# State-space stage of a decoder layer: convolution taps read from PSUM, four banks for the input projection, one pass for all step sizes, and a new order of the two halves

## The reference, cut to what matters

```python
h  = x + mamba2(rmsnorm(x))                       # the state-space stage: this case
h2 = h + silu(n @ gate.T) * (n @ up.T) @ down.T   # n = rmsnorm(h), 1792 inner columns; then x is added
# ... layer norm, cross attention with 8 groups, layer norm, low-rank experts, layer norm

def mamba2(x):
    z, xBC, dt = split(x @ w_in.T, [512, 768, 4])
    xBC = silu(depthwise causal conv over 4 tokens of xBC)       # 6 pieces of 128 channels
    xs, Bs, Cs = split(xBC, [128, 128, 512])
    dt = softplus(dt + dt_bias)                                  # a step size per token and head
    cs = cumsum(dt * A); Ldec = tril(exp(cs_i - cs_j))
    Y = ((Cs @ Bs.T) * Ldec) @ (xs * dt) + D * xs                # per batch and head, 128 tokens
    return (Y * silu(z)) @ w_out.T
```

## Time and profile before

| | us |
|---|---|
| median of 3 runs | 1048.18 |
| the runs | 1047.97 to 1050.05 |
| span of the profiled execution, first to last instruction | 1047.3 |
| PE busy in it | 1001.8 (96%) |
| DVE, ACT, POOL busy | 525.8, 513.7, 434.8 |

### The profile page before, as it was taken

How to read it: one execution, slowest core, us unless ns; L and a number is a source line. 1 busy time by engine, 2 the same in 40 slices (tenths; PEclk the granted TensorE clock), 3 DMA queues, 4 the chain that set the end, 5 groups by cost and what they waited for, 6 DMA issues and landing times.

```text
span 1047.3 us, 16399 instructions
## 1 busy us (share of the span) xinstructions
PE 1001.8 (96%) x5232; PEld 831.5 (79%) x5232; DVE 525.8 (50%) x1229; ACT 513.7 (49%) x1809; POOL 434.8 (42%) x386
## 2 busy tenths in 40 slices
PE   5897998999999998999999999999999999999995
PEld 3664686888888887888888888888888888888772
DVE  4879555122221274445454554545454545545676
ACT  4644443222231347655656555655656556555533
POOL 4435737343443454432623534433433434334311
PEclk9999999999999999999999999999999999999996
DMA  6110114110111112000100110110110110100002
GB/s 209 41 41 0 41 56 146 61 48 12 60 60 60 61 41 74 16 30 38 60 28 12 60 40 0 60 40 0 60 40 20 40 40 20 40 0 1 1 1 81
DMA packets 12832, 45.53 MB, mean 43 GB/s; under 512 B 1600, under 2 KB 2112, under 8 KB 9728
## 3 DMA queue, kind: packets, MB, share of 16 engines
q1 hardware_dynamic: 12800, 45.13, 12.3%
HBM read 43.03 MB, written 2.10 MB: 43 GB/s over the span
## 4 chain that ended last, share of the span: by engine, by line
PE 57%; DVE 2%; POOL 1%; ACT 1%; issue 0%; ACTq 0%
PE bank L349 15%; PE bank L351 15%; PE bank L350 15%; PE bank L621 5%; PE bank L631 3%; PE bank L601 3%; PE bank L708 1%; PE bank L608 1%; POOL w_lo L1264 0%; PE bank L717 0%; DVE bst L1728 0%; PE bank L737 0%; DVE res L1948 0%; POOL pb L1433 0%; PE bank L725 0%
## 5 line engine op out<-in xcount | busy, mean ns | idle before, releaser
L349 PE MATMUL bank<-act_hi,w_hi 128*128 128x512 f32 x560 | 225.8, 403 | 3.9 <-ACT cbuf L838 2.3
L351 PE MATMUL bank<-act_hi,w_lo 128*128 128x512 f32 x560 | 220.9, 395 | 0.0
L350 PE MATMUL bank<-act_lo,w_hi 128*128 128x512 f32 x560 | 220.5, 394 | 0.0
L1422 POOL TENSOR_TENSOR qr<-qv,pow_m 128x4 f32<-128x4 f32 x64 | 64.4, 1007 | 172.3 <-DVE qv L1818 171.0
L349 PEld LDWEIGHTS bank<-act_hi,w_hi 128*128 128x128 f32 x560 | 106.5, 190 | 29.3 <-issue 7.3
L350 PEld LDWEIGHTS bank<-act_lo,w_hi 128*128 128x128 f32 x560 | 106.4, 190 | 24.0 <-issue 2.2
L351 PEld LDWEIGHTS bank<-act_hi,w_lo 128*128 128x128 f32 x560 | 106.4, 190 | 23.4
L1433 POOL TENSOR_TENSOR pb<-pb,prec 128x512 f32<-128x512 f32 x64 | 73.4, 1147 | 109.4 <-DVE prec L1838 109.4
L1829 DVE SCALAR_TENSOR_TENSOR pb<-bank,qr,mask_sb 128x128 f32<-128x128 f32 x256 | 71.9, 343 | 74.2 <-PE bank L621 72.9
L349 PE MATMUL bank<-w_hi,ot_hi 128*128 128x512 f32 x256 | 106.5, 416 | 0.7 <-DVE ot_lo L1498 0.7
L1133 ACT ACTIVATE pb<-pb,nmax 128x128 f32<-128x128 f32 x256 | 100.0, 409 | 9.2 <-DVE nmax L1833 9.2
(11 more groups left out here) (178 smaller groups left out, 2129.4 us busy)
## 6 DMA issues: line engine op xcount, KB each, us to landing
raw_a<-in_w_q SPq DMA_DIRECT2D x8, 1024.0 KB, 4.8
raw_b<-in_w_o SPq DMA_DIRECT2D x8, 1024.0 KB, 4.8
raw_a<-in_w_gu SPq DMA_DIRECT2D x7, 1024.0 KB, 5.2
raw_b<-in_w_kv SPq DMA_DIRECT2D x8, 512.0 KB, 3.3
raw_b<-in_w_dn SPq DMA_DIRECT2D x7, 512.0 KB, 3.4
res<-in_x SPq DMA_DIRECT2D x8, 256.0 KB, 6.2
raw_b<-in_ctx_t SPq DMA_DIRECT2D x8, 256.0 KB, 3.9
xre<-in_x SPq DMA_DIRECT2D x2, 1024.0 KB, 6.8
```

The lines of the kernel that those rows point to most:

```text
L349: mm(o, l_hi, r_hi, start=first, stop=False)
L350: mm(o, l_hi, r_lo, start=False, stop=False)
L351: return mm(o, l_lo, r_hi, start=False, stop=last)
L1422: TT(qr[:, 4 * n + h, :], qv[:, 4 * n + h, :], pow_m[:, 0:HALF], ALU.pow).then_inc(qr_done, 1)
```

## The change: what it does

- DVE's three taps read the projection in its PSUM bank, shifted by 1, 2 and 3 tokens, instead of the padded tile; tile `pre`, its memset and ACT's copy into it (L834) are gone. The bank is free only when the taps are done (conv_c), no longer when ACT has read it (conv_ev).
- The projection goes through banks 4, 5, 0, 1 in turn for f = 0 to 11, then 6, 0, 1, 6, 0, 1, 0, 1.
- All step sizes are worked out in one pass on 32 columns, after the second half's dt_step, in bank 7.
- y_out(0) and y_out(3) no longer stand between the taps of a convolution.
- norm_t 4 to 7 move up, in front of in_step 1 to 4; ssm1(0) comes before in_step(10), the others follow one step earlier; out_step(0) and (1) move between the last in_steps, and norm_t 8 to 12 are spread among the out_steps. ACT, POOL and DVE are reordered to go with it.

```diff
+IN_BANK = [4, 5, 0, 1, 4, 5, 0, 1, 4, 5, 0, 1, 6, 0, 1, 6, 0, 1, 0, 1]
...
     def in_step(f):
-        if f >= 2:
-            pn, pp = order[f - 2]
+        if f == 12:
+            pe.wait_ge(dt_ev, 2)
+        elif f >= 4:
+            before = max(e for e in range(f) if IN_BANK[e] == IN_BANK[f])
+            pn, pp = order[before]
             if pp < NCONV:
-                pe.wait_ge(conv_ev, NCONV * pn + pp + 1)
+                pe.wait_ge(conv_c, NCONV * pn + pp + 1)
             else:
...
     def ssm1(b):
         if b:
             pe.wait_ge(xt_ev, b)
+        else:
+            pe.wait_ge(dt_a, 1)
...
             pe.wait_ge(att_done, b - 1)
+        elif b:
+            pe.wait_ge(z_out, 3)
...
     def in_evac(f):
-            if q >= 2:
-                act.wait_ge(conv_c, q - 1)
-            A(pre[:, q % 2, :, DCONV - 1:], bank[f % 2][:, :].rearrange("p (s n) -> p s n", s=HALF),
-              ACT.Copy)
             if q >= 3:
                 act.wait_ge(conv_out, q - 2)
-            A(cbuf[:, q % 3, :], bank[f % 2][:, :], ACT.Identity,
+            A(cbuf[:, q % 3, :], bank[IN_BANK[f]][:, :], ACT.Identity,
...
-    V.memset(pre[:, :, :, :], 0.0).then_inc(setup_v, 1)
...
-    def conv(q, beside=None):
+    def conv(q):
+        raw = bank[IN_BANK[NPIECE * n + p]][:, :].rearrange("p (s n) -> p s n", s=HALF)
         for k in (2, 1, 0):
-            t = STT(c, pre[:, q % 2, :, k:k + L], cw[:, p * DCONV + k:p * DCONV + k + 1], c,
-                    ALU.mult, ALU.add)
+            late = DCONV - 1 - k
+            t = STT(c[:, :, late:], raw[:, :, 0:L - late], cw[:, p * DCONV + k:p * DCONV + k + 1],
+                    c[:, :, late:], ALU.mult, ALU.add)
...
-    def dt_in(n):
-        bias = sp[:, 6, 0:NH].unsqueeze(1).to_broadcast([P, HALF, NH])
+    def dt_in():
+        bias = sp[:, 6, 0:NH].unsqueeze(1).to_broadcast([P, B, NH])
```

More of the change, by code:

```diff
@@ L444, in _ @@
             dt_step(0)
[L445 to L451, removed]
-            dt_step(1)
+            for i in range(4):
+                norm_t(4 + i, (bank[2], bank[3]))
+                in_step(1 + i)
+            in_step(5)
+            dt_step(1)
+            in_step(6)
+            dt_turn()
+            in_step(7)
+            in_step(8)
+            in_step(9)
+            ssm1(0)
             in_step(10)
-            dt_turn(1)
-            ssm1(0)
+            ssm1(1)
             in_step(11)
-            ssm1(1)
-            in_step(12)
             ssm2(0)
             ssm1(2)
-            in_step(13)
+            in_step(12)
             ssm2(1)
             ssm1(3)
+            in_step(13)
+            ssm2(2)
             in_step(14)
-            ssm2(2)
+            ssm2(3)
             in_step(15)
-            ssm2(3)
             in_step(16)
             in_step(17)
+            out_step(0)
             ssm1(4)
             in_step(18)
+            out_step(1)
             ssm1(5)
@@ L474, in _ @@
             ssm2(4)
-            pe.wait_ge(dt_a, 2)
-            out_step(0)
+            out_step(2)
             ssm1(6)
             ssm2(5)
-            out_step(1)
+            pe.wait_ge(z_out, 8)
+            norm_t(8, tb)
+            out_step(3)
             ssm1(7)
+            norm_t(9, tb)
             ssm2(6)
-            out_step(2)
+            out_step(4)
             ssm2(7)
[L484 to L488, removed]
+            norm_t(10, tb)
+            out_step(5)
+            norm_t(11, tb)
+            out_step(6)
+            out_step(7)
             norm_t(12, tb)
@@ L1287, in _ @@
             TT(qk_w[:, :], chan_sb[:, nq:nq + 1], chan_sb[:, nq + 1:nq + 2], ALU.mult).then_inc(setup_p, 1)
-            for p in range(2, 6):
+            rsqrt(4)
+            win_rest(2)
+            rsqrt(5)
+            win_rest(3)
+            win_rest(4)
+            rsqrt(6)
+            win_rest(5)
+            rsqrt(7)
+            for p in range(6, 10):
                 win_rest(p)
             def decay_in(b):
-                pool.wait_ge(dt_done, b // HALF + 1)
+                pool.wait_ge(dt_done, 1)
                 if b == 0:
@@ L1308, in y_rest @@
                 lo(y_lo[:, b % 4, :, :], yb[:, b % 2, :, :], y_hi[:, b % 4, :, :], ylo_done)
-            for i in range(4, 8):
-                rsqrt(i)
-                win_rest(i + 2)
             decay_in(0)
@@ L1349, in _ @@
             decay_in(6)
+            rsqrt(8)
             decay_out(5)
             decay_in(7)
+            rsqrt(9)
+            y_rest(4)
             gu_rest(0, 0)
-            y_rest(4)
             decay_out(6)
-            rsqrt(8)
+            rsqrt(10)
             y_rest(5)
+            gu_rest(0, 1)
             decay_out(7)
-            gu_rest(0, 1)
-            rsqrt(9)
+            rsqrt(11)
+            y_rest(6)
             gu_rest(0, 2)
-            y_rest(6)
-            rsqrt(10)
             y_rest(7)
+            rsqrt(12)
             gu_rest(0, 3)
-            for i in range(11, 16):
+            for i in range(13, 16):
                 rsqrt(i)
@@ L1700, in _ @@
             rms_var(10)
-            y_out(7)
+            att_mul(6)
+            y_out(5)
+            norm_lo(8, tb)
             add_res(3, 3, OUT_BANK[3])
```

199 lines of the change are left out of this document (97 added, 102 removed).

## The result

| | before | after |
|---|---|---|
| median of 10 runs, us | 1048.99 | 1051.79 |
| the runs | 1047.44 to 1050.05 | 1050.27 to 1053.02 |
| ratio after / before, 95% interval | | 1.0022 [1.0014, 1.003] |
| span of the profiled execution | 1047.3 | 1049.8 |
| its stretches, from dt_step(0) on | 38.22, 38.82, 46.77, 901.33 | 39.55, 38.67, 48.63, 901.30 |

The kernel became slower by 0.2%, 2.8 us. The forecast was 1046.0 us, faster than before, in a range from 1042.0 to 1050.8. The first part of the page and the busy time by stretch answer to the earlier trace rows; the cuts are at the same steps (21.65 behind the first in_step, 61.20 behind in_step(9), 99.87 behind in_step(17), 148.50 the first matmul of the MLP).

What follows compares the result with a forecast made beforehand. PE bounds the kernel, paced by DVE in the first 99 us. Stretch terms +0.8, -4.1 and +1.2 gave -2.1 us: span 1045.2, plus 0.9 to the median, stated as 1046.0 us, range 1042.0 to 1050.8.

Steps and rivals of the forecast that it cites:

- 22.0 + 7.3 + 3.4 + 1.9 = 34.7 ... 4.1 less than before: Second stretch: PE's in_steps, ssm1 and ssm2 steps plus 1.9 us lost at ssm2(3), 4.1 us less than before.
- takes 1.4 (0.1 more for POOL's y_rest(1)): Second stretch, DVE's att(3) ahead of conv(9): 1.4 us, with 0.1 more for POOL's subtraction beside it.
- 40.2 + 3.15 + 1.8 + 1.95 = 47.1: Third stretch: PE's work, pause before out_step(0), its clock, wait at ssm2(7); 0.3 us more than before, 2.1 with the clock.
- the first estimate of what is "lost": First three stretches: time beyond PE's own work, 6.0, 5.7 and 6.6 us, 18.3 us that could be won.
- 1.8 us for each pause from 2 us on: PE after a long pause: matmuls at 1.2 GHz for some nine matmuls, counted as 1.8 us more.
- given back: Rival: the second stretch's gain is given back in full by the pauses, each 0.5 us worse; 1048 us, chance 0.12.
- with 0.9 between span and median: Last term of the sum: 0.9 us added to the span of 1045.2 us to get the median, 1046.1 us.
- The first stretch, +0.8: In_steps 0 to 9: 39.0 us, 0.8 more than before, with PE pausing 4.0 us for xn at norm_t(6).
- The taps: DVE's 36 convolution taps read from PSUM: 0.75 us each instead of 1.055, 11 us less DVE work.
- taps unchanged: Rival: the taps cost in PSUM what they cost now; +5 us, 1051.0 us, chance 0.10.
- the late low parts of w_out: Rival: POOL's low parts come later, holding everything from ssm1(4) on; 1050.7 us, chance 0.16.
- fall DVE's way: Rival: DVE wins the port at rms_x(6) and (7), or w_out is split sooner; 1042.5 us, chance 0.22.

Runs made afterwards that it cites:

- din_late: Changed kernel with POOL's decay_in(4) and decay_in(5) moved behind y_rest(2); 1049.53 us, ratio 1.0007.
- three_edits: Changed kernel with xn of batches 6 and 7 made early, y_out(0) to (2) ahead of conv(7) to (9), out_step(0), (1) behind ssm1(4), (5); 1039.14 us.
- out_late: Changed kernel with PE doing ssm1(4) and in_step(18) ahead of out_step(0), and ssm1(5) ahead of out_step(1); 1046.29 us, ratio 0.9976.
- y_first: Changed kernel with y_out(0), (1), (2) on DVE ahead of conv(7), (8), (9) instead of behind them; 1050.37 us, ratio 1.0012.
- xn_early: Changed kernel with the squares, rms_var, rsqrt and rms_x of batches 6 and 7 moved earlier on ACT, DVE and POOL; 1043.81 us, ratio 0.9954.
- taps_alone: Kernel before with the taps from PSUM and the new banks, old order and two step-size passes kept; 1040.59 us, ratio 0.992.
- pool_port: Changed kernel with POOL doing win_rest(5) ahead of rsqrt(6) and win_rest(6) ahead of rsqrt(7); 1051.31 us, ratio 1.003.
- four_edits: Changed kernel with xn early, y_out ahead of conv, out_step(0), (1) behind ssm1, and decay_in(4), (5) behind y_rest(2); 1040.15 us, ratio 0.9904.

## Why the prediction was wrong

**What failed first: the second stretch, "22.0 + 7.3 + 3.4 + 1.9 = 34.7 ... 4.1 less than before".** Measured, 38.67. The step of it was "takes 1.4 (0.1 more for POOL's y_rest(1))". DVE's timeline over two batches:

```profile
77.56 0.69 DVE L1627 TENSOR_TENSOR att<-em,bank 128x512 f32<-128x512 f32 x1 [0.58 <-PE bank L433]
78.29 1.46 DVE L1629 TENSOR_TENSOR att<-att,diag_d 128x512 f32<-128x512 f32 x1
79.67 2.29 DVE L1574 SCALAR_TENSOR_TENSOR cbuf<-bank,cw,cbuf 128x508 f32<-128x508 f32 x3
81.87 0.68 DVE L1637 TENSOR_TENSOR yb<-zt,bank 128x512 f32<-128x512 f32 x1
84.66 1.48 DVE L1629 TENSOR_TENSOR att<-att,diag_d 128x512 f32<-128x512 f32 x1
86.05 2.28 DVE L1574 SCALAR_TENSOR_TENSOR cbuf<-bank,cw,cbuf 128x508 f32<-128x508 f32 x3
88.26 0.68 DVE L1637 TENSOR_TENSOR yb<-zt,bank 128x512 f32<-128x512 f32 x1
```

and POOL's beside it:

```profile
83.29 1.29 POOL L1278 TENSOR_TENSOR y_lo<-yb,y_hi 128x512 fp32r<-128x512 f32 x1 [2.34 <-ACT y_hi L895]
84.55 1.03 POOL L1321 TENSOR_TENSOR md<-dt_sb,cst 128x512 f32<-128x512 f32 x1
```

The walk saw y_rest (until 84.6) and let att's second product go on behind it. But decay_in(5) follows at once, and the product that began at 84.66 took 1.48 us, until 0.56 after decay_in's end. That is 0.75 where 0.1 was counted, and it lies in a loop: y_out, ssm2, att, convolution, y_out. The forecast has 5.5 us for a turn of it; measured, two turns (76.33 to 82.70 and on to 89.08) took 6.4 each. PE has 5.5 us of work in the first of them and only 3.6 in the second, where no ssm1 stands: hence the pauses of 0.70 and 2.53. Behind the second the clock fell, which cost 1.6 more. In din_late, with decay_in elsewhere, the product takes 0.69, a turn 5.6 (75.54, 81.13, 86.73), and the stretch 35.42. Of the 4.0 us that the stretch is too long, then, 0.7 are the first pause, 0.6 the longer second one, 1.6 the clock, and 0.5 PE's own work, which is 33.2 at full clock (three_edits) and not 32.7; the rest is spread.

**What failed with it: the third stretch, "40.2 + 3.15 + 1.8 + 1.95 = 47.1".** It was walked on from in_step(17) ending at 95.85, so din_late, where that nearly came true, is its test: 50.27 us, 3.5 more than before, against +0.3 to +2.1. PE's own work is some 41.5 us and not 40.2 (41.64 busy in three_edits, 41.32 in out_late, both at full clock); the pause before out_step(0) was 3.53 (3.15), its clock 2.5 (1.8), ssm2(7) 1.55 (1.95), and out_step(4) waited 1.23 for add_res, which the walk didn't have. So with the second stretch as forecast the kernel would still not have been faster than before: din_late is at 1049.53, ratio 1.0007 [0.9997, 1.0016]. In the changed kernel the third stretch measured +1.86, inside its range, and that is luck: PE came late, so the pause was only 2.75 with 1.6 of clock, which made up in part for add_res and for PE's work. The low count of PE's work is in the first estimate of what is "lost" as well: of the 6.6 us only some 5.3 were to be had (46.77 less 41.5). The price of a fall of the clock, "1.8 us for each pause from 2 us on", came out at 1.5, 1.6 and 1.6 in the changed kernel, but other runs have pauses over 2 us without a fall (last section).

The rival "given back" had the direction of this, and put it at 1048; in the changed kernel there was no gain in the second stretch to give back. The edits show how far it goes: y_first wins 4.8 and gives 4.4 back, din_late 1.6 of 3.25, xn_early nothing of 6.8.

**The last term, "with 0.9 between span and median".** Every run on record lies 1.8 us above its own span, the changed kernel's median 2.0 above the span of its profile. The 0.9 came from a median of three runs, 1048.18; ten runs give 1048.99. That is 1.1 of the 5.8 us between 1046.0 and 1051.79. The other 4.6 lie in the span: 4.0 in the second stretch, 0.5 in the first, 0.7 in the third, less 0.5 by the earlier start.

**The first stretch, +0.8: measured +1.33, mechanism right.** Xn of batch 6 began at 32.85 (33.35 forecast), took 1.74 with win_rest(5) in its way, PE paused 3.68 (4.0) with the clock low behind it, norm_t(7) 1.12 (1.15), in_step(9) ended at 61.20 (61.1). The stretch is 0.5 longer than forecast because it began 0.5 earlier and still ended where the walk has it. Up to norm_t(7) the distances are the walk's (19.06 us, 18.99 forecast); the 0.5 are lost behind it, where eight transposes took 0.68 (0.35 forecast for the turn) and an in_step 2.77 instead of 2.75. What the walk didn't say is that all this was the price of an order: xn_early takes 6.8 us out of it by moves on three engines.

**The taps: right, and misjudged in their place.** 0.74 us each whatever POOL does, 11.3 us less DVE work as forecast (11). A part of it went to products that POOL now blocks: up to 149 us the 14 xn take 14.7 us (15 took 12.6 before), att's second products 7.6 (6.6). In the old order the taps shorten the first two stretches by 9.3 us (taps_alone). The forecast priced no version without the new order. Measured side by side, the new order with its one pass for the step sizes costs 10.7 us (1051.75 against 1041.05).

**Of the rivals** "taps unchanged" came nearest in time (1051.0), and is out, with taps of 0.74. Next came the late low parts of w_out (1050.7): they did end late, at 102.73 instead of 99.0, but PE was late too, so the pause at out_step(0) was 2.75, not longer than the 3.15. The port did not fall DVE's way (xn took 1.74 and 1.76); pool_port gets a short xn by another order, with the block on conv_silu(1) instead, so what that rival is worth stays unmeasured. None of the three signs that were to show the prediction wrong came (taps of 1.05, no wait at norm_t(6), none at out_step(0)): they watched single mechanisms, and the sum failed.

**Open.** By the ratios against the changed kernel, with some 2 us of doubt on each, xn's place bears 7 us, out_step(0)'s 5 and y_out's 1; together they measured 12. How this compares move by move with the old order was not tried. One pass for all step sizes was not tried alone in the old order, nor the padded tile in the new one. Ssm1(4)'s 2.6 us for conv_silu(11) are still there in the fastest version.

## What to carry to other kernels

Where engines hand a tile round in a loop, add up one turn of the loop, with what the neighbouring engine does next and not only now, and compare it with the bound engine's work in that same turn: 0.75 us of a blocked product decided 3 us here. A gain ahead of a wait is lost at that wait unless what releases it gets earlier too (y_first kept 0.4 of 4.8 us, xn_early all of 6.8), so look for the next releaser and ask where it stands. And price a change that has a cheap part and a reordering separately; here the part alone was worth 0.8%, and the whole cost 0.2%.

## What the runs showed of the hardware

- A DVE operation with two inputs in SBUF that begins while one on POOL is under way ends 0.54 to 0.56 us after POOL's end, nine times of nine in the changed kernel from 30 to 140 us: att's second product at 86.14 behind decay_in's 85.58, xn (32.85, 1.74 us) at 34.59 behind a w_lo subtraction's 34.04 (32.78, 1.26 us). POOL's next operation therefore counts as much as its present one. Taps with one input in PSUM lie between 733 and 749 ns, all 36, with no such case.
- PE's clock, by pauses: after 1.77 us (din_late, ssm2(3)) and 1.87 the next matmuls ran at 2.4 GHz; after 1.98, 2.35 (pool_port), 2.53 and 2.75 (changed kernel) entries of 1.2 GHz follow. But after 2.57 in three_edits and 2.67 in pool_port they do not, and after 2.57 in four_edits they do: in this range the length of a pause alone doesn't tell. Where the clock fell, it cost 1.5 to 1.7 us behind pauses up to 3.68, and 2.5 behind those of 3.53 (din_late), 4.3 (taps_alone) and 6.12 (y_first).
- Spans of single profiled executions differ more than the effects at issue: the part behind the state-space stage, the same code in all kernels, took 898.46 us in xn_early and 903.73 in pool_port. Only medians of several runs beside the kernel before, and stretches whose waits have been read, bear a conclusion here.
